# A graph attention network on one core: chunks begun in two passes, columns by pieces, reorders, and a softmax with one exponential

## What is computed

```
def gat_conv(x, src, dst, W, a_src, a_dst, b, heads, out_ch):
    h = (x @ W).reshape(n, heads, out_ch)
    alpha_src = jnp.einsum('nhc,hc->nh', h, a_src)
    alpha_dst = jnp.einsum('nhc,hc->nh', h, a_dst)
    e = jax.nn.leaky_relu(alpha_src[src] + alpha_dst[dst], 0.2)
    m = jax.ops.segment_max(e, dst, num_segments=n)
    p = jnp.exp(e - m[dst])
    denom = jax.ops.segment_sum(p, dst, num_segments=n)
    alpha = p / denom[dst]
    msg = h[src] * alpha[:, :, None]
    return jax.ops.segment_sum(msg, dst, num_segments=n).reshape(n, heads * out_ch) + b
```

## Time and profile before

| | us |
|---|---|
| median of 3 runs (lowest, highest) | 380.62 (380.08, 380.71) |
| the profiled execution | 379.96 |
| its span, first to last instruction | 378.2 |
| busy: TensorE, Vector, ACT, GpSimd | 357.7, 218.0, 214.8, 248.1 |
| mean granted TensorE clock, share of full | 0.997 |

### The profile page before, as it was taken

One profiled execution on the slowest core, in us unless ns is written; L12 is line 12 of the kernel. 1 busy time (PEld: TensorE's weight loads), 2 busy tenths in 40 slices (PEclk: granted clock), 3 DMA queues, 4 the chain that ended last, 5 costly groups with the idle time before them and its releaser, 6 DMA issues.

```text
span 378.2 us, 6192 instructions
## 1 busy us (share of the span) xinstructions
PE 357.7 (95%) x2103; PEld 306.3 (81%) x2106; DVE 218.0 (58%) x563; ACT 214.8 (57%) x374; POOL 248.1 (66%) x171
## 2 busy tenths in 40 slices
PE   6999888999999999999999999998789999899992
PEld 2888787988988988898898898897567888688882
DVE  3697777318236345543741832836665787944866
ACT  4993458756665664773765665564553657245501
POOL 2777707776946948749668686690459876577911
PEclk9999999999999999999999999999999999999998
DMA  7967944637527545754662753755253365355002
GB/s 266 346 193 231 332 196 122 224 124 256 190 87 221 201 160 168 220 194 117 218 240 91 250 170 111 248 184 164 64 188 110 88 179 172 146 168 167 2 0 83
DMA packets 24544, 65.15 MB, mean 172 GB/s; under 512 B 1952, under 2 KB 3024, under 8 KB 24528
## 3 DMA queue, kind: packets, MB, share of 16 engines
q1 hardware_dynamic: 20720, 55.19, 44.4%
q10 hardware_dynamic: 3808, 9.76, 8.1%
HBM read 64.15 MB, written 0.79 MB: 172 GB/s over the span
## 4 chain that ended last, share of the span: by engine, by line
PE 72%; ACT 7%; DVE 6%; issue 6%; POOL 4%; DMA 3%; SPq 1%; POOLq 0%; ACTq 0%; DVEq 0%
PE ps L908 51%; PE ps L1151 8%; PE ps L999 6%; POOL ring_lo L360 3%; ACT ring_hi L347 2%; PE ps L1017 2%; DMA x_sb<-in_x 2%; DMA raw<-in_L_gnn_W 2%; PE ps L972 1%; PE ps L1212 1%; ACT rows_hc L684 1%; POOL x_sb L613 1%; ACT z L684 1%; ACT am L684 1%; PE ps L958 1%
## 5 line engine op out<-in xcount | busy, mean ns | idle before, releaser
L360 POOL TENSOR_TENSOR ring_lo<-raw,ring_hi 128x768 fp32r<-128x768 f32 x94 | 170.8, 1852 | 78.5 <-ACT ring_hi L347 78.5
L347 ACT ACTIVATE ring_hi<-raw 128x768 fp32r<-128x768 f32 x96 | 77.5, 851 | 32.6 <-PE ps L908 28.6
L376 POOL TENSOR_TENSOR ring_lo<-raw,ring_hi 128x512 fp32r<-128x512 f32 (+1 forms) x40 | 59.7, 1523 | 30.6 <-ACT ring_hi L369 30.6
L1341 DVE CUSTOM_DVE_ANT_0 e<-ps,att 128x768 f32<-128x768 f32 (+1 forms) x56 | 41.9, 801 | 53.7 <-PE ps L908 51.1
L908 PE MATMUL ps<-ring_hi,zT_hi 128*128 128x512 f32 (+1 forms) x256 | 69.4, 346 | 1.1 <-DVE zT_lo L1497 1.1
L908 PE MATMUL ps<-ring_hi,zT_lo 128*128 128x512 f32 (+1 forms) x256 | 67.4, 338 | 0.0
L908 PE MATMUL ps<-ring_lo,zT_hi 128*128 128x512 f32 (+1 forms) x256 | 67.3, 338 | 0.0
L908 PE MATMUL ps<-ring_hi,xT_hi 128*128 128x512 f32 x192 | 51.8, 346 | 0.1
L908 PE MATMUL ps<-ring_lo,xT_hi 128*128 128x512 f32 x192 | 51.0, 342 | 0.0
L908 PE MATMUL ps<-ring_hi,xT_lo 128*128 128x512 f32 x192 | 50.6, 340 | 0.0
L908 PEld LDWEIGHTS ps<-ring_lo,zT_hi 128*128 128x128 f32 x256 | 43.1, 188 | 5.7
(11 more groups left out here) (157 smaller groups left out, 554.0 us busy)
## 6 DMA issues: line engine op xcount, KB each, us to landing
raw<-in_L_gnn_W SPq DMA_DIRECT2D x54, 768.0 KB, 4.4
raw<-in_L_gnn_Wr SPq DMA_DIRECT2D x8, 768.0 KB, 4.4
...
```

The lines of the kernel that those rows point to most:

```text
L347: eng.activation(slot_hi(c), raw_chunk(c), ACT.Copy).then_inc(hi_done, 1)
L360: eng.tensor_tensor(slot_lo(c), raw_chunk(c), slot_hi(c).bitcast(F32), ALU.subtract)\
L376: eng.tensor_tensor(ring_lo[:, q["ring_at"]:q["ring_at"] + w], raw[:, q["raw_group"], q["raw_at"]:q["raw_at"] + w], ring_hi[:, q["ring_at" ...
L1341: dve.tensor_tensor_reduce(junk[:, at:at + w], of[:, (k - first_head(a)) * w:(k - first_head(a) + 1) * w], att[:, half_at * row + k * w:ha ...
```

## The change

It does the following.

- *Softmax.* a_dst is now scaled by -0.8. ACT writes 0.2 s - 0.8 d for each tile (`leaks`, Identity with a bias and a scale) as soon as scores and dots are there; Vector takes the maximum with s (`leaky_scores`), then adds `far`, negates and takes the minimum in place (`tile_tops`), and ACT makes one exponential per tile. Tiny operations, second exponentials and their maxima are gone. In a head, Vector's h_lo is split around the minima; `far`, counts and exps of head 0 are ordered anew, and counts are ACT's.
- *Two passes first.* Head 0's chunk 0 starts after the first transposes of x, with the passes that need no lo part of x; the other two groups of transposes stand before chunks 1 and 2. The same for the first two chunks of `last_accumulate` and of the first wide product; `aggregate_T` begins its first quarter with the hi weights, `aggregate` each tile.
- *Column pieces.* conv2's last projected tile is dotted in 512 and 256 columns; its aggregate goes by 512 and 256 columns, with bias and statistics by the same pieces.
- *Reorders.* One-hot rows around `input_lo`; scores(0) in front of the second half of the counting; ELU of head 0; x1 of tile 0 on Vector; `biased_half(1, 1)` after the first h1 tile; the last layer's centre, statistics and shift interleaved.

The diff, cut to its core (declarations, counts of semaphores, head 0's bookkeeping and the ELU's order left out):

```diff
@@ scalar
+            def leaks(a):
+                act.wait_ge(scores_bc, a + 1)
+                for i in range(NT):
+                    act.wait_ge(a_dst_done, before(a) + heads_of(a) * (i + 1))
+                    for k in range(heads_of(a)):
+                        at = s_at(a, k)
+                        act.activation(e1[:, first_head(a) + k, i, :], ps[:, at:at + N], ACT.Identity,
+                                       bias=a_d[:, pair(a, k, i)], scale=SLOPE).then_inc(leak_done, 1)
...
             def exps(a, order):
-                act.wait_ge(bias_done, 2 * a + 2)
...
+                for n, i in enumerate(order):
+                    act.wait_ge(masked, before(a) + heads_of(a) * (n + 1))
+                    for k in range(heads_of(a)):
+                        at = masked_at(a, k, i)
+                        act.activation(at, at, ACT.Exp, bias=top[:, pair(a, k, i)], scale=-1.0).then_inc(e_done, 1)
...
             def softmax_and_elu(h, last=False):
+                leaks(h)
                 projected_hi(h)
                 exps(h, (1, 0))
...
+            split_hi(act, FIRST_PHASE, 0, reused=False)
+            input_hi(0)
+            split_hi(act, FIRST_PHASE, 1, reused=False)
+            split_hi(act, FIRST_PHASE, 2, reused=False)
+            input_hi(1)
             act.wait_ge(iota_cast, 2)
             act.wait_ge(self_cast, 1)
             ramps(ET, ET + NT)
             split_hi(act, FIRST_PHASE, 3, reused=False)
+            input_hi(2)
...
-            layer_norm(0, 0, x_sb[:, 0, :], y[0])
@@ vector
+            def leaky_scores(a):
...
+                dve.wait_ge(leak_done, before(a) + NT * n)
+                for i in range(NT):
+                    for k in range(n):
+                        at = s_at(a, k)
+                        dve.tensor_tensor(masked_at(a, k, i), ps[:, at:at + N], e1[:, first_head(a) + k, i, :], ALU.max)\
+                           .then_inc(leaky_done, 1)
+            def tile_tops(a, i):
...
+                    dve.tensor_tensor_reduce(at, at, far[:, i, :], -1.0, 3.0e38, ALU.add, ALU.min, top[:, pair(a, k, i)])\
+                       .then_inc(masked, 1)
...
             def softmax(h):
-                masked_scores(h)
-                projected_lo(h)
+                leaky_scores(h)
+                dve.wait_ge(leaky_done, 2 * h + 2)
+                projected_lo(h, 0)
+                for i in (1, 0):
+                    tile_tops(h, i)
+                projected_lo(h, 1)
                 normalised(h)
                 weights_lo(h)
...
             tile_dots(A_CONV2, 0)
             conv2_lo(0)
-            tile_dots(A_CONV2, 1)
+            dve.wait_ge(wide_piece_done, 1)
+            piece_dots(slice(N, D), None, (partial_done, partial_done))
+            projected(A_CONV2, 1)
+            dve.wait_ge(partial_done, 2)
+            piece_dots(slice(0, N), partial, (a_src_done, a_dst_done))
...
+            y_piece(0, 0)
+            y_piece(0, 1)
+            y_stats(0)
+            y_piece(1, 0)
+            x1(0)
+            y_piece(1, 1)
+            y_stats(1)
             x1_lo(0, 0)
             x1_lo(0, 1)
+            x1(1)
...
             layer_mean(1, 0, 3 * NT + 1)
-            biased_half(1, 1)
-            layer_mean(1, 1, 3 * NT + 2)
             h1_centre(0, 0)
             h1_centre(1, 0)
             h1_scale(0, 0)
             h1_add(0, 0)
             h1_scale(1, 0)
+            biased_half(1, 1)
+            layer_mean(1, 1, 3 * NT + 2)
+            h1_lo(0, 0)
             h1_centre(0, 1)
...
+            out_stats(0)
+            out_centre(0)
+            out_stats(1)
+            out_shift(0)
+            out_centre(1)
+            out_shift(1)
@@ tensor
+            transpose_x(0)
             for c in range(CH):
...
+                if c in (1, 2):
+                    transpose_x(c)
+                if c == 0:
+                    pe.wait_ge(xT_hi_done, 1)
+                    chunk(FIRST_PHASE, 0)
+                    for passes in (FIRST_TWO, LAST_ONE):
+                        if passes is LAST_ONE:
+                            pe.wait_ge(xT_lo_done, 1)
...
             for c in range(CH):
                 if c == 2:
                     pe.wait_ge(b1_ready, 2)
                     count_edges(0, COUNT_HALF)
+                    scores(0)
                     count_loops()
                     count_edges(COUNT_HALF, ET)
-                if c == 3:
-                    scores(0)
...
+            pe.wait_ge(z_hi_done, 3 * (H0 - 1) + 1)
+            for c in (0, 1):
+                chunk(PHASES - 1, c)
+                last_accumulate(c, 0, passes=FIRST_TWO)
+            pe.wait_ge(z_lo_done, 3 * (H0 - 1) + 1)
+            for c in (0, 1):
+                last_accumulate(c, 0, passes=LAST_ONE)
...
+            pe.wait_ge(x1T_hi_done, 1)
+            for q in w1a[:2]:
+                wide_product(q, 0, 0, passes=FIRST_TWO)
+            pe.wait_ge(x1T_lo_done, 1)
+            for q in w1a[:2]:
+                wide_product(q, 0, 0, passes=LAST_ONE)
+            transpose_x1(1)
```

306 lines of the change are left out of this document (161 added, 145 removed).

## The result

The changed kernel takes 374.0 us (median of four executions, 373.21 to 374.96) against 380.35 beside it: ratio 0.983, 95% interval 0.980 to 0.987, so 6.35 us less where 4.3 were predicted. The forecast of 376.3 and even the low end of its range, 374.2, lie above it.

What follows compares the result with a forecast made beforehand. TensorE, busy 357.7 of 378.2 us, was taken to bound the kernel, so only its waits counted. Eight terms (1.4 + 0.2 + 0 + 0 + 0.75 - 0.75 + 1.25 + 1.45) gave 4.3 us off 380.62: 376.3, range 374.2 to 379.3.

Steps and rivals of the forecast that it cites:

- Term 1: Start: chunk 0 begins after the first transposes of x, at the low clock either way; 1.4 us gained, bounds 0 to 2.6.
- Term 2: Heads 0 and 1: shorter ELU chain mostly given back to the new softmax; 0.2 us gained, bounds 0 to 0.8.
- Term 3: Heads 2 to 7: the new softmax still fits, 0.5 us to spare; nothing gained, bounds 0 to -3 us.
- rival (b): Steady heads overrun their slack and each of six heads waits; 382 at 1.75 us of chain growth; chance 0.09.
- Term 4: Last accumulate: may begin earlier but then waits for the next zT_lo; nothing gained, bounds 0 to 0.2.
- Term 5: Second convolution to x1: earlier statistics, gain limited by GpSimd's splits; 0.75 us gained, bounds 0 to 1.9.
- Term 6: First GAT layer's softmaxes: half A unchanged, half B makes TensorE wait; 0.75 us lost, bounds 0 to -1.5.
- Term 7: h1: first tile ready earlier, 0.3 given back at the second; 1.25 us gained, bounds 0 to 1.5.
- Term 8: Tail: tile 1's centre and shift moved into Vector's wait; 1.45 us gained, bounds 0.5 to 1.6.
- (a): Front and middle give nothing, leaving terms 6 to 8 and little else, 2.3 us gained: 378.3; chance 0.22.
- (c): More than reckoned: term 1 at 2.6, x1(0) and x1(1) both 0.5 earlier, half B hidden: 374.2; chance 0.10.

Runs made afterwards that it cites:

- before_fill: The kernel before, with six and four fillers (matmuls on zeros) in TensorE's two gaps between the transposes of x: 378.10 us, ratio 0.995.
- start_old: The changed kernel with the start of the kernel before put back (all three transposes of x ahead of chunk 0): 376.43 us, ratio 0.990.
- elu_old: The changed kernel with head 0's old ELU order and the old aggregate_T put back: 374.62 us.
- slack_over: The changed kernel with two extra copies of 128x512 on ACT between the two leaks of heads 2 to 6: 376.37 us.
- root_first: The changed kernel with GpSimd's root of tile 0 of x1 moved ahead of its lo parts of chunks 3 to 5: 376.45 us.
- pool_waits: The changed kernel with GpSimd waiting for x1(1) before it splits wide chunks 6 to 8: 373.99 us, ratio 0.984.
- shift_spread: The changed kernel with ACT's start reordered, GpSimd waiting for x1(1), and GpSimd's bias sum and shift tiles spread into its own gaps: 371.27 us, ratio 0.978.
- h1_only: The kernel before with only the new order of h1 on Vector: 379.26 us, ratio 0.9966.
- tail_only: The kernel before with only the new order of the last layer's statistics, centre and shift: 379.18 us, ratio 0.9962.

## Why the prediction was wrong in size and right in sign

**Term 1, predicted 1.4: the step that failed.** In the first profile it is 1.14 (counting at 27.89, predicted 27.5; wait of 1.2 for chunk 4, predicted 0.7). But the step "it runs at the low clock either way" took the clock of one row of before as a property of the place. It hangs on the two idle stretches ahead of it, of 1.4 and 1.0 us, which the change removes: filled, they leave chunk 0 at 2.4 GHz (before_fill), and put back, they bring the clock down again (start_old). Where TensorE goes from the fillers to chunk 0 with only 0.7 us of idleness it is at 2.4 GHz in most executions, and the start gives 2.99 us (weights(0) at 41.91 against 44.90). start_old measures 3.1. That is 1.6 above the forecast of the term at the lower level, where the whole miss is some 2.7 (380.35 less 373.33 less 4.3); at the median of the first four executions, between the levels, the miss is 2.05. The bound of 2.6 for this term was worked out with the low clock inside it, and so was the end of the range.

**Term 2, predicted 0.2.** 0.68 by the leads of the first profile (1.14 at weights(0), 1.82 when head 2 begins). The 0.83 of the ELU order is there, elu_old shows it, and so is the wait at weights(1), 0.65 instead of 0.9. At weights(1) 0.24 of the 0.83 is left (the lead is 1.38), and the stall at 73.6, gone as reckoned, adds 0.44, where 0.2 were forecast.

**Term 3, predicted 0.** 30.40 us a head before and after, no wait; slack 0.5 predicted, 0.47 measured. The mechanism of rival (b) is real, as slack_over shows; its condition was not met.

**Term 4, predicted 0.** The lead is 1.82 before and 1.84 after the last accumulate. TensorE waits 0.4 at its beginning and 0.5 for zT_lo at chunk 2.

**Term 5, predicted 0.75.** 1.38: the lead grows from 1.84 to 3.22 at the second transposes of x1. inverse_root(0, 0) does stand right behind a GpSimd split, as predicted, but at 277.77 and not at 278.1 (279.9 less the lead), and x1(0) takes 0.68, not 0.87: I had priced one instruction of 768 columns as two of 384. x1(1) went the other way, 1.60 against 1.34 in the earlier trace rows. Both run beside GpSimd's splits from start to end, so what differs is the point at which x1(1) meets a split: it starts 0.36 us behind a split's start in before (284.95), 0.09 behind in the changed kernel (281.74) and 0.07 and 0.06 behind in root_first, and takes 1.34, 1.60, 1.62 and 1.61. It ends 1.67 to 1.70 us behind that split's start every time.
The Trainium skill (SBUF — State Buffer, SBUF: two separate sides) calls this pair an exclusive lock: whichever of a Vector instruction in a two-port mode and a GpSimd instruction starts first has it, and the other is blocked. The durations fit that: 0.68 of its own and up to 0.9 of waiting inside a GpSimd split of 1.27 us, and the later it comes, the less it waits. The other side pays too: GpSimd's split behind it takes 1.59. By that rule the cost is up to one GpSimd instruction, not a share of bandwidth, where the forecast had taken 0.45 for a meeting that it called possible. That this instruction is in a two-port mode no run here shows.

**Term 6, predicted -0.75.** -0.6, but in two places. Half B lost 0.3 (the lead falls from 2.91 at its scores to 2.61 at its weights), since ACT's ring splits end at 306.3, 309.2 with the lead added, and not at 309.6. Half A lost 0.3, where I had none: TensorE stood at chunk 11 until GpSimd's lo part of it was done (from the scores of half A at 292.45 to its weights at 302.33 it needs 9.88 us, and 9.57 in before). pool_waits and shift_spread show what holds it: the GpSimd queue with the tail's work in it.

**Term 7, predicted 1.25.** 1.5 at the first h1 tile (2.61 to 4.11), 0.45 given back at the second (0.3 predicted): 1.05. Alone, in h1_only, 1.3.

**Term 8, predicted 1.45.** 5.0 us from the tile-0 sum to the last mean, 1.44 gained; 1.45 alone, in tail_only.

In the frame of the first profile the eight terms come to 1.14 + 0.68 + 0 + 0 + 1.38 - 0.6 + 1.05 + 1.44 = 5.1 against 5.0 of span. So the sum, worked out for an execution with the low clock, was 0.7 off: terms 2 and 5 gave 1.1 more than reckoned, term 1 gave 0.3 less; and the forecast was for a kind of execution that one in three turned out to be. Executions of that kind, at 374.7 to 375.0, lie inside the stated range.

Two sums of the rivals do not come out as written. In (a) terms 6 to 8 leave 1.95 and not 2.3, so 378.7. In (c) the gains named are 1.2, 0.5 and 0.75, so 373.9 and not 374.2, and (c), held at 0.10, came nearest. It has the right places and not the reason: its start is at the 2.6 of the low clock.

The effect of the clock could have been seen before: the rows have 0.64 a pair, the page showed full clock, and I asked what the pairs cost and not why they were slow.
